# Three of the four channel tiles of a Mamba block's convolution in two token phases, in a one-core Trainium2 megakernel

## The reference

```
xc, z = split(x @ in_proj.T)                    # 512 channels each
u  = conv over 4 taps of xc, all 512 x 512 channels, causal, plus bias
dt = clip(sigmoid(u @ dt_w.T + dt_b), 1e-4, 1)
B, C = u @ B_w.T, u @ C_w.T                     # 16 columns each
per token: state = exp(dt * A) * state + dt * B * u + 1e-6
           y = sum over the 16 states of state * C, plus D * u
x = x + (y * silu(z)) @ out_w.T
```

## Time and profile before

| what | value |
|---|---|
| time before, median of 3 runs | 1473.14 us |
| the profiled execution, its own time | 1464.08 us |
| its span on the core | 1462.3 us |
| mean granted TensorE clock | 0.975 of full speed |
| PE / DVE / ACT / POOL busy | 93% / 70% / 64% / 59% of the span |
| first scan of batch 0, 1, 7 starts; last scan starts | 462.5, 555.8, 1153.6; 1252.4 us |

### The profile page before, as it was taken

One profiled execution on the slowest core, in us unless ns is written; L12 is line 12 of the kernel. 1 busy time (PEld: TensorE's weight loads), 2 busy tenths in 40 slices (PEclk: granted clock), 3 DMA queues, 4 the chain that ended last, 5 costly groups with the idle time before them and its releaser, 6 DMA issues.

```text
span 1462.3 us, 22311 instructions
## 1 busy us (share of the span) xinstructions
PE 1363.0 (93%) x7072; PEld 959.2 (66%) x7072; DVE 1017.6 (70%) x1535; ACT 934.8 (64%) x1735; POOL 868.0 (59%) x440
## 2 busy tenths in 40 slices
PE   5899997999999999999999999999999788889997
PEld 2566686999764555565655655656556576569996
DVE  6666635333344899899898998998998988853332
ACT  1222232344326999999998998999999998114442
POOL 1110002555211898898898898988988878325552
PEclk9999999999999999999999999999999978999999
DMA  9400014766420797998997988989979978376662
GB/s 297 162 29 27 17 31 145 212 207 209 151 70 23 168 219 176 197 220 183 202 224 178 213 191 193 222 188 198 224 165 206 240 188 194 83 237 211 207 208 80
DMA packets 108229, 248.39 MB, mean 170 GB/s; under 512 B 19097, under 2 KB 49950, under 8 KB 94048
## 3 DMA queue, kind: packets, MB, share of 16 engines
q0 software_dynamic: 23104, 131.96, 41.7%
q1 hardware_dynamic: 82944, 113.68, 25.6%
q10 hardware_dynamic: 2080, 1.47, 0.3%
HBM read 116.72 MB, written 18.94 MB: 93 GB/s over the span
## 4 chain that ended last, share of the span: by engine, by line
PE 68%; ACT 17%; DVE 9%; issue 4%; DMA 2%; POOL 0%; DVEq 0%; POOLq 0%; ACTq 0%; SPq 0%
PE ps L1366 11%; PE ps L1579 10%; PE ps L1588 9%; ACT arena L781 7%; PE ps L1699 7%; ACT arena L791 7%; PE ps L1668 5%; PE ps L1391 4%; PE ps L1741 3%; PE ps L1730 3%; DVE arena L1241 2%; PE ps L1428 2%; PE ps L1685 2%; PE ps L1382 2%; PE ps L1497 2%
## 5 line engine op out<-in xcount | busy, mean ns | idle before, releaser
L530 POOL TENSOR_TENSOR arena<-arena 128x2048 f32<-128x2048 f32 x91 | 424.9, 4685 | 107.3 <-DVE arena L1241 102.6
L1366 PEld LDWEIGHTS ps<-cst,arena 128*128 128x128 f32 x2428 | 299.7, 145 | 279.3 <-issue 190.9
L1241 DVE TENSOR_TENSOR_SCAN arena<-arena,ps 128x512 f32<-128x512 f32 x364 | 431.9, 1210 | 62.4 <-PE ps L1366 55.0
L1366 PE MATMUL ps<-cst,arena 128*128 128x128 f32 x2428 | 370.4, 281 | 50.3 <-ACT arena L791 23.8
L781 ACT ACTIVATE arena<-arena,a_neg 128x512 f32<-128x512 f32 x512 | 366.1, 715 | 40.7 <-DVE arena L1241 30.0
L791 ACT ACTIVATE arena<-arena,m_bt 128x512 f32<-128x512 f32 x510 | 361.8, 710 | 2.0 <-PE ps L1366 1.1
L1668 PE MATMUL ps<-arena,tapw 128*128 128x512 f32 x448 | 224.5, 595 | 0.0
L1241 DVE TENSOR_TENSOR_SCAN x<-arena,ps 128x512 f32<-128x512 f32 x148 | 175.6, 1209 | 19.8 <-PE ps L1366 18.4
L530 POOL TENSOR_TENSOR x<-x,arena 128x2048 f32<-128x2048 f32 x36 | 170.1, 4734 | 13.4 <-DVE x L1241 13.2
L1114 DVE TENSOR_TENSOR arena<-ps,arena 128x256 f32<-128x256 f32 x78 | 33.2, 425 | 201.5 <-PE ps L1588 195.9
L477 POOL DMA_INDIRECT arena<-rows,arena x78 | 75.7, 971 | 157.6 <-DVE arena L1094 134.4
(11 more groups left out here) (173 smaller groups left out, 1628.8 us busy)
## 6 DMA issues: line engine op xcount, KB each, us to landing
arena<-arena POOLq DMA_DIRECT2D x52, 1024.0 KB, 8.3
arena<-in_W SPq DMA_DIRECT2D x94, 512.0 KB, 4.3
arena<-c_rows SPq DMA_DIRECT2D x128, 256.0 KB, 3.7
arena<-x POOLq DMA_DIRECT2D x28, 1024.0 KB, 8.4
x<-arena POOLq DMA_DIRECT2D x24, 1024.0 KB, 8.2
rows<-x SPq DMA_DIRECT2D x16, 512.0 KB, 4.3
x<-residual SPq DMA_DIRECT2D x12, 512.0 KB, 5.9
x<-in_x SPq DMA_DIRECT2D x8, 512.0 KB, 11.2
```

What stands on the lines that cost most here:

```text
L530: g.tensor_tensor(h, h, m_c[i % RC].unsqueeze(1).to_broadcast([P, KI, SEQ]), ALU.mult)\
L1241: v.tensor_tensor_scan(out=h[:, k, :], data0=m_a[g % RA], data1=ps[SCAN_BANK[g % 3]][:, :], initial=0.0, op0=ALU.mult, op1=ALU.add).then_i ...
L1366: return t.transpose(bank, src[:, k * P:(k + 1) * P], ident)
```

## The change

- **Convolution.** For batches 1 to 7, tile 0 stays as it was. Tiles 1, 2 and 3 take the three-part form: 12 matmuls of 256 columns each in place of 8 of 512. `m_both` and `m_join` now run for them too, at `UC_AT` and `JOIN_AT`. POOL makes the differences once per batch (`m_differ`, two instructions of 512 columns, after the C product of state 15) and the tap sums once (two instructions, before the first scan).
- **Space.** The differences lie in chunks 4 to 7 of x and the tap sums in chunks 8 to 15, so the ring of four is gone. SP loads the rows for the norm at state 6 (`N_LOAD`) into chunks 4 to 7, and those for the update at state 2 into chunks 0 to 3: two loads of 512 KB per batch in place of one. Before batch 7, batches 4 and 5 are read back from HBM into the convolution's weights' space, as is the last batch's x.
- **Order.** All the tables are new. The y banks are (4, 5, 4, 5). `m_bcmm` waits for all four tiles of u. C row 14 of batch 7 is loaded beside row 15 into a space of its own.
- **Start.** DVE signals each normalised chunk of sequence 0 and PE turns it at once (`a_turn_first`); ACT issues one small Exp before it waits for the weights; the statistics of the last 16 chunks are spread: two after each of the four bias pairs, five before the mask, and the last three and the scales after the mask.

The diff, cut to its core ("..." marks what is left out):

```diff
-CONV_AT = ((0, 1, 2, 2, 3, 4, 5, 6), (7, 8, 8, 10, 11, 12, 13, 14), (14, 15, 16, 17, 18, 20, 21, 21), (22, 23, 24, 26, 28, 29, 30, 30))
-UT_AT = (12, 19, 25, 34)
-OUT_AT = ((23, 25, 25, 26, 28, 29, 32, 33), (38, 39, 41, 43, 43, 47, 49, 49))
-BC_AT = (19, 23, 27, 34)
-DT_AT = ((33, 34, 36, 36), (37, 38, 39, 40), (43, 44, 45, 47), (48, 49, 50, 51))
-DTT_AT = (40, 44, 50, 55)
-BT_AT = 41
+CONV_AT = ((0, 1, 1, 2, 3, 4, 5, 6), (5, 6, 7, 7, 9, 9, 10, 10, 11, 11, 12, 13), (14, 14, 15, 15, 15, 16, 16, 16, 17, 17, 18, 18), (19, 20, 20, 20, 20, 21, 21, 21, 22, 22, 23, 23))
+UT_AT = (12, 17, 25, 28)
+OUT_AT = ((22, 24, 24, 24, 27, 28, 28, 31), (36, 38, 38, 40, 41, 43, 45, 47))
+BC_AT = (26, 27, 29, 30)
+DT_AT = ((31, 32, 33, 33), (34, 35, 36, 37), (42, 42, 42, 43), (45, 46, 47, 49))
+DTT_AT = (38, 40, 51, 54)
+BT_AT = 39
 SPIN_AT = (59, 61, 62)
-C_STORE = 10
-Z_AT = ((52, 53), (54, 55), (56, 57), (58, 59))
-XT_AT = (52, 53, 55, 57)
-
-
-UC_AT = (10, 18, 25, 32)
-UTC_AT = (12, 21, 31, 36)
-BCC_AT = 35
-TH_AT = (37, 41, 47, 52)
+C_STORE = 9
+N_LOAD = 6
+JOIN_AT = (14, 19, 24)
+Z_AT = ((52, 53), (55, 55), (56, 58), (58, 59))
+XT_AT = (51, 52, 55, 59)
+
+
+UC_AT = (8, 10, 17, 21)
+UTC_AT = (12, 19, 29, 31)
+BCC_AT = 36
+TH_AT = (35, 38, 45, 50)
 ZTH_AT = (54, 56, 58, 60)
-NORM_AFTER = (9, 10, 11, 12)
-XTC_AT = (61, 63)
-
-
-ADD_AT = ((7, 8, 10, 15), (12, 14, 14, 17))
-FINAL_AT = (13, 15, 17, 21)
-UPDATE_AT = (34, 50)
-STAT_AT = (36, 38, 58, 63)
-SKIP_AT = (3, 5, 8, 16)
-CLIP_AT = (38, 42, 48, 52)
-WT_AT = (40, 45, 51, 56)
-BTC_AT = 44
-GATE_AT = (55, 57, 59, 61)
-
-
-XT_BANK, CONV_BANK, UT_BANK, OUT_BANK = (0, 7), (0, 1, 0, 1), (0, 1, 0, 1), (4, 5)
-BC_BANK, BT_BANK, DT_BANK, DTT_BANK, Z_BANK, Y_BANK = 7, 7, (0, 1, 0, 1), (0, 1, 0, 1), (4, 5, 4, 5), (4, 5, 7, 4)
+NORM_AFTER = (8, 10, 11, 12)
+DIFFER_AFTER = 15
+XTC_AT = (60, 62)
+
+
+ADD_AT = ((8, 9, 15, 18), (12, 13, 16, 19))
+FINAL_AT = (13, 15, 18, 20)
+UPDATE_AT = (31, 52)
+STAT_AT = (33, 37, 62, 63)
+SKIP_AT = (2, 4, 14, 17)
+CLIP_AT = (35, 38, 47, 51)
+WT_AT = (39, 41, 50, 58)
+BTC_AT = 39
+GATE_AT = (54, 56, 59, 60)
+
+
+XT_BANK, CONV_BANK, UT_BANK, OUT_BANK = (7, 0), (0, 1, 0, 1), (0, 1, 0, 1), (4, 5)
+BOTH_BANK = 7
+BC_BANK, BT_BANK, DT_BANK, DTT_BANK, Z_BANK, Y_BANK = 7, 7, (0, 1, 0, 1), (0, 1, 0, 1), (4, 5, 4, 5), (4, 5, 4, 5)
...
+        m_xd = x[:, CPB:2 * CPB, :].rearrange("p c d -> p (c d)").rearrange("p (s k t) -> p s k t", s=2, k=KD)
+        tap_sum = x[:, 2 * CPB:4 * CPB, :].rearrange("p c d -> p (c d)").rearrange("p (j k n) -> p j k n", j=2, k=KD)
...
-                    if n == 2 and 2 <= b < BATCH - 2:
-                        new = b + RING - 2
+                    if n == 2 and b >= 2:
                         sp.wait_ge(S("f1_rows"), 16 * (b - 1))
                         if b > 2:
-                            sp.wait_ge(S("ld_again"), 16 * (b - 2))
-                        sp.dma_start(x[:, kept(new):kept(new) + CPB, :],
-                                     x_mid[new * SEQ:(new + 1) * SEQ].rearrange("(c p) d -> p c d", p=P))\
-                            .then_inc(S("ld_again"), 16)
+                            sp.wait_ge(S("ld_late"), 16 * (b - 2))
+                        sp.dma_start(x[:, 0:CPB, :], x_mid[(b - 1) * SEQ:b * SEQ].rearrange("(c p) d -> p c d", p=P))\
+                            .then_inc(S("ld_late"), 16)
+                    if n == N_LOAD and b < BATCH - 2:
+                        sp.wait_ge(S("m_umm"), conv_done(b + 1, KI - 1))
+                        if b:
+                            sp.wait_ge(S("ld_rows"), 16 * b)
+                        sp.dma_start(x[:, CPB:2 * CPB, :],
+                                     x_mid[(b + 2) * SEQ:(b + 3) * SEQ].rearrange("(c p) d -> p c d", p=P))\
+                            .then_inc(S("ld_rows"), 16)
+                    if n == NS - 2 and b == BATCH - 2:
+                        sp.wait_ge(S("m_umm"), conv_done(BATCH - 1, KI - 1))
+                        sp.wait_ge(S("f1_rows"), 16 * (BATCH - 2))
+                        for k in range(RING, BATCH - 2):
+                            sp.dma_start(staged[k], xs[1][k * SEQ:(k + 1) * SEQ, 0:D].rearrange("(c p) d -> p c d", p=P))\
+                                .then_inc(S("ld_back0"), 16)
+                        sp.wait_ge(S("ld_rows"), 16 * (BATCH - 2))
+                        sp.dma_start(x[:, CPB:2 * CPB, :], x_mid[(BATCH - 1) * SEQ:BATCH * SEQ].rearrange("(c p) d -> p c d", p=P))\
+                            .then_inc(S("ld_rows"), 16)
                     if b == BATCH - 1 and n == NS - 4:
                         sp.wait_ge(S("f_tr"), BATCH + FEED_ORDER[1].index(2) + 1)
+                        sp.wait_ge(S("m_zmm"), KI * (BATCH - 1))
+                        sp.dma_start(c_last, c_rows[b % 2][NS - 2].partition_broadcast(P)).then_inc(S("m_c_end"), 16)
...
+            def m_differ(n):
+
+                g.wait_ge(S("m_xtc"), KD * (n + 1))
+                for s in range(2):
+                    g.tensor_tensor((m_xd if n else xd_first)[:, s], m_xt[n % 2][:, :, PAD + 1 - 2 * s:PAD + SEQ - 2 * s:2],
+                                    m_xt[n % 2][:, :, PAD:PAD + SEQ - 1:2], ALU.subtract).then_inc(S("m_xd"), 1)
+
+            m_differ(0)
+            g.wait_ge(S("m_stat0"), 2)
+            for j in range(2):
+                sum_taps(tap_sum, j)
+            m_differ(1)
 
...
                 if i % NS >= 2 and i < BATCH * NS - 4:
                     add_on(i)
+                if i % NS == DIFFER_AFTER and i // NS < BATCH - 2:
+                    m_differ(i // NS + 2)
...
+            a.wait_ge(S("set"), 2)
+            a.activation(a_nr[:, 0:HPT], zero_row[:, 0:HPT], ACT.Exp)
...
+            def m_both(n, o):
+
+                a.wait_ge(S("m_umm"), conv_done(n, o, BOTH_END))
                 if n >= 2:
                     a.wait_ge(S("m_y0"), KI * (n - 2) + o + 1)
-                a.activation(m_u[n % 2][:, o, :], ps[CONV_BANK[o]][:, :], ACT.Identity, bias=mvec[:, 0, o:o + 1])\
-                    .then_inc(S("m_u"), 1)
...
-                if k == 3:
-                    a.wait_ge(S("m_y"), KI * b + 1)
+                else:
+                    a.wait_ge(S("m_y"), KI * b + k - 1)
...
                     v.wait_ge(S("a_tr"), b)
+                if isinstance(b, int) and b == 0:
+                    for c in range(CPB):
+                        ln_apply(a_xn[:, c, :], c).then_inc(S("a_xn0"), 1)
+                    return
                 for c in range(CPB):
...
                     v.tensor_tensor(a_k[:, c, :], ps[4 + c % 2][:, 0:D], bkv[:, 0:D], ALU.add).then_inc(S("a_kb"), 1)
+                    for i in rows[2 * c:2 * c + 2]:
+                        row_stats(i)
...
+                later = range(2 * CPB + EARLY, NCH)
+                a_kvbias(b, () if before else later[0:2 * CPB])
                 a_qfeature(b)
                 a_kfeature(b)
-                if not before:
-                    first_stats(2 * CPB + EARLY, NCH, 2 * CPB)
                 if before:
                     a_update(b - 1)
+                else:
+                    for i in later[2 * CPB:-LATE]:
+                        row_stats(i)
                 a_mask(b)
+                if not before:
+                    for i in later[-LATE:-1]:
+                        row_stats(i)
+                    link(row_stats(NCH - 1))
+                    layer_norm_scales(2 * CPB, NCH)
 
...
+            def m_join(n, o):
+
+                v.wait_ge(S("m_both"), both_done(n, o))
+                if n and o == 1:
+                    v.wait_ge(S("m_u"), KI * n + 1)
+                v.wait_ge(S("m_umm"), conv_done(n, o))
+                u = m_u[n % 2][:, o, :].rearrange("p (t s) -> p t s", s=2)
                 v.tensor_tensor(u, ps[CONV_BANK[o]][:, :].rearrange("p (s t) -> p t s", s=2),
                                 u[:, :, 1].unsqueeze(2).to_broadcast([P, HALF, 2]), ALU.add).then_inc(S("m_u"), 1)
...
+                if q in JOIN_AT:
+                    m_join(n, JOIN_AT.index(q) + 1)
...
+            def a_turn_first():
+                for c in range(CPB):
+                    t.wait_ge(S("a_xn0"), c + 1)
+                    for k in range(KD):
+                        last = turned(ps[k][:, c * P:(c + 1) * P], a_xn[:, c, :], k, c)
+                last.then_inc(S("a_tr"), 1)
+
...
+            def m_conv(n, o, i):
+
+                if n and o == 0:
+                    d, k = i // TAPS, i % TAPS
+                    if k == 0:
+                        t.wait_ge(S("m_xtc"), KD * n + 2 if i == 0 else KD * n + d + 1)
+                    mm = t.matmul(ps[CONV_BANK[0]][:, :], tapw[:, k, d, 0:P], m_xt[n % 2][:, d, k:k + SEQ],
+                                  start=(i == 0), stop=(i == TAPS * KD - 1))
+                    if i == TAPS * KD - 1:
+                        mm.then_inc(S("m_umm"), 1)
+                    return
...
                 if o == 1 and i == 0 and n >= 2:
                     t.wait_ge(S("m_wt"), KI * n)
```

(26 more changed lines are left out.)

152 lines of the change are left out of this document (70 added, 82 removed).

## The result

| | kernel before | changed kernel |
|---|---|---|
| median of 20 executions each, us | 1471.38 (1463.22 to 1486.69) | 1483.81 (1469.21 to 1493.4, and one of 1993.97 at a mean clock of 0.648) |
| the profiled execution, its span, mean clock | 1464.08, 1462.3, 0.975 | 1477.05, 1475.3, 0.960 |

The ratio is **1.0063, 95% interval 1.0038 to 1.0089**: slower by 0.6%, 9 us, where 1451.3 us and a gain of 21.8 us were forecast. The sign is wrong. The ratios here are taken over the executions within 1.5% of their kernel's fastest (19 of 20 before, 18 of 20 after), so they are not the ratios of the medians.

The account below looks back on a forecast made before the run. PE was taken to lead the scan batches (96.52 of 99.70 us busy), ACT and DVE close behind, DVE fullest in slots 8 to 15. Terms 16.5 - 1.5 + 6.8 = 21.8 us; 1473.1 - 21.8 = 1451.3 us, range 1436 to 1466.

Parts of the forecast that it names:

- Batch 0's 1.5: Batch 0, which also prepares by the new convolution form: 1.5 us gained, from 0.6 to 4.4.
- I take 1.5 us lost, from a gain of 1 to a loss of 6: End of batch 6 and batch 7: extra loads ahead of C row 15 and the later update cost 1.5 us net.
- both of my prices: Landing times at the end of batch 6: 10.4 us for a 512 KB load, 3.6 us for a C row.
- The update at slot 52: Batch 7: update at slot 52 instead of 50, PE waiting for it at slot 53; no separate size given.
- 2.5 us less: Batches 1 to 6: 97.1 us each in place of 99.6, ends 0.5 and 4.4; 15 us for the six.
- the idle time of the leader, 4.2 us forecast: Each scan batch: three nearly equal engines near 92.9 us, plus 4.2 us idle, give 97.1 us.
- ACT's third skip waiting for the first final: Closing of y: ACT's `m_skip` at slot 14 waits for DVE's first `m_final` at slot 13; counted inside the 4.2 us.
- The start's 6.8 us: Before and in the first attention: earlier copies 1.1, earlier mask 4.1, faster `a_attend` 2.1, less 0.5; range 4 to 7.5.
- ACT and DVE bind at once: Rival, scan part: these engines or extra DMA traffic limit the gain to 0.5 us per batch, 3.6 in all; 1464 us; chance 0.22.
- The clock rival: Rival, batches 1 to 6: more PE idleness lowers the clock to batch 7's 0.83, 11 us more each; 1532 us; chance 0.05.
- 0.91 for faster: Whole kernel: chance 0.91 of being faster by more than 4.4 us (0.3%), within it 0.04, slower 0.05.
- three terms: Whole kernel: 16.5 us gained in batches 0 to 6, 1.5 lost to moved waits and loads, 6.8 gained at the start.

Follow-up runs that it names:

- experiment 1: Changed kernel with batch 6's loads moved: batch 4's rows and the last x at state 7, batch 5's rows after C row 15; 1467.92 us, ratio 1.0008 to the kernel before.
- experiment 3: Experiment 1 with the first closing of y a slot earlier (FINAL_AT 12 in place of 13); 1470.79 us, ratio 1.0021 to the kernel before.
- experiment 6: Changed kernel without batch 5's read-back (router takes its rows from x first), batch 4's rows and last x loaded at state 7; 1474.17 us, ratio 1.0018.
- experiment 4: Experiment 1 with four idle matmuls of 256 columns in slot 15; 1463.87 us, ratio 0.9975 (0.9942 to 1.0007) to the kernel before.
- experiment 9: Changed kernel without batch 5's read-back, with idle matmuls at slot 15 and in the logits stage; 1470.54 us, ratio 1.0007 to the kernel before.
- experiment 11: Changed kernel with the old start, no read-back of batch 5 and slot 15's idle matmuls; median 1469.72 us, ratio 0.9981 to the kernel before.
- experiment 12: Changed kernel with its new start, no read-back of batch 5 and slot 15's idle matmuls; median 1468.38 us, ratio 1.0017 to the kernel before.
- experiment 5: Changed kernel with nothing but four idle matmuls of 256 columns ahead of slot 15's spread; 1474.11 us, ratio 1.0043 to the kernel before.
- experiment 2: Kernel before with only the new start (chunks turned one by one, early Exp, spread statistics); 1470.74 us, ratio 1.0009 to the kernel before.
- experiment 10: Changed kernel with the start of the kernel before, so the scan part alone; 1477.79 us, ratio 1.0066 to the kernel before.

## Why the prediction was wrong

Between the profiles, a forecast gain of 21.8 us stands against a loss of 13.0. Batch 7 is 15.0 us of the difference, batches 1 to 6 are 11.3, the way from the span's start to the first scan 7.7, and what follows the last scan 0.7. Batch 0's 1.5 came as forecast, which says little: with the new form it took 91.1 to 94.4 us in the other versions.

- **"I take 1.5 us lost, from a gain of 1 to a loss of 6" is the step that failed most**: batch 7 lost 16.5 us in the profile, and moving the loads alone (experiment 1) took the ratio from 1.0063 to 1.0008, 8 us; between the two profiles batch 7 shortened by 5.8. I had named the place but followed only what is behind the waiting SP, C row 15. I did not ask who reads what SP fetches: `x_turn` in slot 2 needs both read-backs, and PE carries the scans. And both of my prices were medians over a whole batch, not taken from the moment at which the loads fall. The changed kernel's DMA issues in batch 6 (KB each, median us to landing) show the read-backs at 14.7, not 10.4, and the last C row took 17.68, not 3.6 plus 6:

```profile
x<-arena POOLq DMA_DIRECT2D x13, 1024.0 KB, 9.5
arena<-c_rows SPq DMA_DIRECT2D x16, 256.0 KB, 3.8
...
tapw<-rows SPq DMA_DIRECT2D x2, 512.0 KB, 14.7
```

- The loss is not all of one wait. Where the slot-2 stand was taken away, batch 7 stayed at 104 to 111 us. In experiments 1, 3 and 6 the closing of y waited for the even sum, and that goes back to the moved loads: they held C row 8 of batch 6, and POOL with it, by 10 us. In experiments 4, 9, 11 and 12 that row landed after 12.0 to 13.6 us and POOL waited 4.5 to 6.0; batch 7 took 103.9 to 109.9. The update at slot 52, which the prediction had named and put inside the 1.5 us, holds PE for 2.7 us in all of them. Where the clock was at 1.00 there, slots 48 to 55 took 13.1 us, and 16.9 where it was 0.74. The DMA share around the end of batch 6 is 1.02 to 1.04 in the kernel before too, without the extra loads. No run with the new convolution had its last batches without the extra loads, so what they cost in all stays open. The kernel before is not steady there either: in its four profiles with this scan part batch 7 took 97.4, 100.0, 106.4 and 106.5 us, by the landing of one read-back and by the clock. So "16.5 us" has a spread of its own.
- **"2.5 us less" per batch**: 0.6 on average in the changed kernel's profile, 1.5 where the clock held (experiments 4, 5, 11). The loads were right: PE 92.1 forecast and 91.7 measured, DVE 92.8 and 92.1, ACT 92.9 and 92.6, POOL 89.2 and 89.0; the matmul of 256 columns takes 0.43 us, not 0.45. What was off is the idle time of the leader, 4.2 us forecast, 98.0 - 92.6 = 5.4 measured. I summed over the batch; the batch is a sum of stretches, each as long as its own fullest engine. Slots 0 to 7 grew from 10.9 to 11.8 us (more convolution on a full PE) and slots 8 to 15 stayed at DVE's load. The earlier trace rows showed DVE at 13.80 of 14.00 there, and I had quoted it. The other 1.1 us, in five of the six batches, is the clock after PE's stand of 1.9 us, shown by experiment 5. That stand is the chain which the prediction did name, ACT's third skip waiting for the first final, and put inside the 4.2.
- **The start's 6.8 us**: 5.4 came, where the prediction had put it: `a_attend` starts 3.8 us earlier (39.94, forecast near 38.6) and takes 2.0 less. But "after it the loop over sequences is full on PE, so the gain stays" is wrong. It was there at the query of sequence 7 and lost by the first scan. Experiment 2 shows no gain from the start alone, and experiment 10 shows the same loss as the changed kernel without the new start. In the profiles the logits stage took 28.0, 30.4 and 28.0 us with the old start (the kernel before and experiments 10 and 11) and 31.4, 31.6 and six times 43 to 45 with the new one (experiments 1 to 6). So the long form came in six of eight profiles with the new start and in none of three with the old one. The executions agree: six of experiment 2's 12 have a mean clock under 0.968, against three of 35 of the kernel before beside it, and its times go with the clock, from 1455.28 us at 0.978 to 1482.99 at 0.962. The new start makes the lower clock more frequent, then. It is not the only way to it (experiment 10 has 0.92 in the stage with the old start), and what in the start does it was not found.
- **The rivals.** The first ("ACT and DVE bind at once", 0.5 us a batch, 1464) had the scan part's size right and its reason nearly: DVE binds, in one stretch. It missed batch 7 as the forecast did. The clock rival was not what happened, the mean clock of batches 1 to 6 being 0.98 or 1.00, but the clock took 1.1 us in most batches and at least the 3.4 us of the logits stage before the scans, and I had given it no term at all. In the prediction the Trainium skill's "TensorE: Matmul & The Clock Gate" (section on oscillation) stood for idle stretches that bring the lower level back. Batch 3 agrees; batch 2, with the same 1.9 us, does not; and in the kernel of experiment 2 the profile shows PE busy all the time at half clock:

```profile
202.00:212.00 10.00, 10.00 (x37) 8.14 (x38) 0.00 (x0) 1.48 (x4) 0.00 (x0) 0.50 0.13 2
```

- **The chances.** 0.91 for faster rested on three terms that could all be smaller but hardly negative; a wait of PE on a transfer that the kernel before did not need had no case of its own. It should have been the rival on the other side.

## What to carry to other kernels

When a buffer is given up and its rows are fetched again, look for the first reader of the fetched rows, and price the fetch by transfers at that moment, not by the median of a batch. Ask also what is issued behind it on the same engine: a load moved to a quieter place (experiment 1) made the row behind it 14 us late there. A gain on the leading engine is to be summed stretch by stretch, each with its own fullest engine, before it is multiplied by the number of batches. A few microseconds saved in front of a stage can shift or change the clock in it; measure the part alone before counting it.
